# Gathers of a four-layer graph network: staged loops and a 12-batch ring against unrolled gathers, a 16-batch ring, and a ramp in PSUM

## What is computed

```
L0:  agg = segment_sum(relu(h[src]), dst); relu(relu((h+agg) @ W1 + b1) @ W2 + b2)
L1:  4 times: a = segment_sum((feat @ W[etype]^T + b[etype])[src], dst)
     feat = gru(a, feat)
L2:  twice: h = h @ W; out = segment_sum(h[src] * norm, dst) + b     (with self loops)
L3:  h = [x_i, x_j - x_i] @ W^T + b for each edge (i = dst, j = src)
     batch norm over all edges, leaky relu, mean over the edges of each dst
```

## Time and profile before

| | |
|---|---|
| median of three runs | 18,841.41 us (18,836.34 to 18,843.33) |
| profiled execution: its span, first to last instruction | 21,319.6 us |
| the profiled execution's own time outside the span | not given; its time is at least the span |
| POOL busy | 13,832.9 us, 65% |
| TensorE matmul / weight load busy | 10,388.0 us / 8,431.9 us |
| VectorE / ScalarE busy | 4,301.6 us / 813.3 us |
| DMA engines' mean busy share, moved | 0.09 + 0.04, 656 MB |

### The profile page before, as it was taken

How to read it: one execution, slowest core, us unless ns; L and a number is a source line. 1 busy time by engine, 2 the same in 40 slices (tenths; PEclk the granted TensorE clock), 3 DMA queues, 4 the chain that set the end, 5 groups by cost and what they waited for, 6 DMA issues and landing times.

```text
span 21319.6 us, 182142 instructions
## 1 busy us (share of the span) xinstructions
PE 10388.0 (49%) x40885; PEld 8431.9 (40%) x40886; DVE 4301.6 (20%) x4825; ACT 813.3 (4%) x2691; POOL 13832.9 (65%) x13640
## 2 busy tenths in 40 slices
PE   3333544445444463444634445443544445666689
PEld 2333333334333343333433333333433334656678
DVE  2111121112111121111211113111211112111168
ACT  0000000001000010000100001000000000000000
POOL 6766557774677746777377764676567764666677
PEclk5555555555555555555555555555555555555555
DMA  1111011110111111111111100111011111222222
GB/s 40 22 22 22 17 40 22 23 22 28 29 23 23 23 35 22 22 23 23 35 22 23 23 21 18 22 23 23 21 23 23 23 22 35 66 66 66 66 63 64
DMA packets 739325, 656.19 MB, mean 31 GB/s; under 512 B 457733, under 2 KB 467541, under 8 KB 738918
## 3 DMA queue, kind: packets, MB, share of 16 engines
q0 software_dynamic: 407168, 419.46, 9.4%
q1 hardware_dynamic: 332134, 236.47, 3.9%
HBM read 532.79 MB, written 122.26 MB: 31 GB/s over the span
## 4 chain that ended last, share of the span: by engine, by line
POOL 36%; another core or an unknown queue 25%; issue 19%; PE 15%; DVE 3%; DMA 1%; DVEq 1%; ACT 1%; POOLq 0%; ACTq 0%; SPq 0%
POOL HG L479 30%; PE ps L722 7%; POOL HG L461 5%; PE ps L875 2%; PE ps L803 2%; PE ps L719 1%; DVE OH L1012 1%; PE ps L766 1%; DMA HG<-tab_edge,STG 1%; PE ps L866 1%; DVEq L1005 1%; PE ps L835 0%; ACT RZ L643 0%; DMA HG<-tab_gin,STG 0%
## 5 line engine op out<-in xcount | busy, mean ns | idle before, releaser
L722 PE MATMUL ps<-HG,OH 128*128 (+2 forms) x26560 | 6212.0, 421 | 5999.6 <-issue 2938.7
L722 PEld LDWEIGHTS ps<-HG,OH 128*128 128x128 f32 x26560 | 5859.6, 329 | 6909.3 <-issue 6907.0
L479 POOL DMA_INDIRECT HG<-tab_gated,STG x6252 | 6424.0, 1028 | 2729.0 <-issue 2037.4
L479 POOL DMA_INDIRECT HG<-tab_gcn,STG x3126 | 3192.7, 1021 | 1386.1 <-issue 942.1
L1008 DVE TENSOR_TENSOR A<-A,ps 128x640 f32 (+1 forms) x1328 | 1091.9, 822 | 14010.3 <-issue 13934.3
L719 PE MATMUL ps<-ZERO 1*128 1x512 bf16 (+1 forms) x3819 | 1543.4, 535 | 3677.8 <-issue 2629.8
L461 POOL DMA_INDIRECT HG<-tab_gin,STG x1660 | 1712.9, 1032 | 750.3 <-issue 514.8
L461 POOL DMA_INDIRECT HG<-tab_edge,STG x1660 | 1587.9, 957 | 879.0 <-issue 490.4
L719 PEld LDWEIGHTS ps<-ZERO 1*128 1x128 bf16 x3819 | 338.8, 114 | 4260.3 <-issue 4199.7
L1012 DVE TENSOR_TENSOR OH<-IOTAR,DLOC 128x1280 f32<-128x1280 f32 x1328 | 2002.5, 1508 | 0.3 <-DVE A L1130 0.2
L875 PE MATMUL ps<-A,HG 128*128 (+1 forms) x3320 | 733.8, 353 | 601.6 <-issue 493.8
(11 more groups left out here) (157 smaller groups left out, 3002.8 us busy)
## 6 DMA issues: line engine op xcount, KB each, us to landing
HG<-tab_gated,STG POOLq DMA_INDIRECT x6252
A<-dloc_dram SPq DMA_DIRECT2D x166, 320.0 KB
kept<-HG SPq DMA_DIRECT2D x166, 320.0 KB
HG<-kept SPq DMA_DIRECT2D x166, 320.0 KB, 2.9
tab_gated<-TW SPq DMA_DIRECT2D x196, 256.0 KB, 2.0
HG<-tab_gcn,STG POOLq DMA_INDIRECT x3126
HG<-tab_gin,STG POOLq DMA_INDIRECT x1660
HG<-tab_edge,STG POOLq DMA_INDIRECT x1660
```

Source lines behind the costliest of these rows:

```text
L479: nc.gpsimd.indirect_dma_start(out=RINGF[:, at:at + D], out_offset=None, in_=table, in_offset=bass.IndirectOffsetOnAxis(ap=STG[:, h, u:u + ...
L722: return nc.tensor.matmul(ps[:, base:][:, bass.ds(place, width)], onehots_, rows_, start=False, stop=False, skip_group_check=True)
```

## The change

- The ramp for the one-hots is copied once into the last bank of PSUM (`ps_ramp`), and both comparisons read it, or a lane number (`ps_lane`), from there. `turned_onehots` is a tensor-tensor comparison now.
- The host lays out the index tables by row (`src_cols`, `type_cols`), so IDX and IDX4 are filled by two plain loads and some arithmetic; the indirect DMAs take their indices straight from them. STG, the staging copies and two of the three transposed tables are gone; the 13 fetches of the prologue bring only `dst`.
- All eight passes use one `gather` over 1,563 rows, unrolled (no hardware loop), into a ring of 16 batches. Before batch b it waits for the landing of batch b-2 and, from batch 16 on, for group b-5 (REACH is 11; `product`, or `e_joined` in the edge pass).
- In the first pass the ring's pitch is 65, with a column of ones for the counts, and the sums start from the normalised x. In the edge pass the join is ten additions, each from its ring slot (registers), into OH.
- The prologue normalises x and writes the first table before the edge rows are dealt with. Chunk buffers share one tensor (TEMP), lists lie in one tensor at four partitions.

```diff
-RING = 12
+RING = 16
+REACH = (GRP - 1 + NB - 1) // GRP + 1
...
+        ps_ramp = ps[:, 4096 - P:4096]
+        ps_lane = ps[:, 4095 - P:4096 - P]
...
+            def gather(n, table, index, pitch, rows, ring, freed, freed_before):
+                for b in range(BATCHES):
+                    h = b % 2
+                    if b >= 2:
+                        pool.wait_ge(rows[h], rows_before(ring, h) + (b // 2) * (16 * GRP))
+                        pool.sem_inc(pool_go, 1)
+                    if b >= RING:
+                        pool.wait_ge(freed, freed_before + min(b - RING + REACH, 2 * TRIPS))
+                        pool.sem_inc(pool_go, 1)
+                    for k in range(b * GRP, min((b + 1) * GRP, ROWS)):
+                        at = (k % RING_ROWS) * pitch
                         nc.gpsimd.indirect_dma_start(
                             out=RINGF[:, at:at + D], out_offset=None, in_=table,
-                            in_offset=bass.IndirectOffsetOnAxis(ap=STG[:, h, u:u + 1], axis=0)
+                            in_offset=bass.IndirectOffsetOnAxis(ap=index[:, k:k + 1], axis=0)
                         ).then_inc(rows[h], 16)
-                with pool.Fori(0, LAPS) as lap:
-                    for j in range(RING):
-                        batch(lap, j, GRP)
-                batch(LAPS, 0, ROWS - LAPS * RING_ROWS)
...
-            gather(0, tab_gin, rows_other, False)
+            gather_sums(0, tab_gin, IDX, D + 1, rows_other, 0)
...
-                gather_ring(step + 1, step, tab_gated, rows_gated)
+                gather_sums(step + 1, tab_gated, IDX4, D, rows_gated, step)
...
-                gather_ring(STEPS + 1 + k, STEPS + k, tab_gcn[k], rows_other)
+                gather_sums(STEPS + 1 + k, tab_gcn[k], IDX, D, rows_other, k + 1)
...
-            gather(LAST_PASS, tab_edge, rows_other, True)
+            gather(LAST_PASS, tab_edge, IDX, D, rows_other, 3, e_joined, 0)
...
-                def stage(i, h):
-                    nc.scalar.copy(STG[:, h, :], group_cols(IDX4, i, h)).then_inc(staged[h], 1)
...
             def onehots(cols, h):
-                return V.tensor_tensor(OH[:, h, :, :], IOTAR[:, :].unsqueeze(1).broadcast_to([P, GRP, P]),
+                return V.tensor_tensor(OH[:, h, :, :], ps_ramp.unsqueeze(1).broadcast_to([P, GRP, P]),
                                        cols.unsqueeze(2).broadcast_to([P, GRP, P]), ALU.is_equal)
...
-                V.tensor_scalar(OTS[:, h, :, :], DROW[:, h, :, :], VIS[:, 0:1], None, ALU.is_equal
-                                ).then_inc(e_turned, 1)
+                V.tensor_tensor(OTS[:, h, :, :], DROW[:, h, :, :], ps_lane.unsqueeze(1).broadcast_to([P, GRP, P]),
+                                ALU.is_equal).then_inc(e_turned, 1)
...
             def join(g, h, i):
+                rows = load_rows(g)
+                needed = dve.value_load(LOC[0:1, bass.ds(g * LPG + GRP, 1)], min_val=1, max_val=BATCHES)
                 dve.wait_ge(e_picked, g + 1)
...
-                dve.wait_ge(rows_other[h], rows_before(2, h, 1) + (i + 1) * (16 * GRP))
-                V.tensor_tensor(G[:, h, :, 0:D], G[:, h, :, 0:D], ps_u[:, h, 0:GRP, :], ALU.add).then_inc(e_joined, 1)
+                dve.wait_ge(batch_in, LAST_PASS * BATCHES + needed)
+                for u in range(GRP):
+                    ins = V.tensor_tensor(JOINED[:, h, u, 0:D], RINGF[:, bass.ds(rows[u], D)], ps_u[:, h, u, :],
+                                          ALU.add)
+                ins.then_inc(e_joined, 1)
...
             dve.wait_ge(typ_in, 32)
...
+            V.scalar_tensor_tensor(IDX4[:, :], IDX[:, :], float(TYPES), IDX4[:, :], ALU.mult, ALU.add
+                                   ).then_inc(idx_set, 1)
+            rescale(0, FEAT, SUMS)
 
             dve.wait_ge(rows_in, 16 * VT)
```

More of the change, by code:

```diff
@@ L24 @@
+import math
 from contextlib import ExitStack
@@ L204, in gnn_kernel @@
+        TOTAL = TEMP[:, 3 * GRP * P:3 * GRP * P + P]
+        JOINED = OH
+        LOADED, SCALED, ACTED = (cut(RINGF, k * 2 * GRP * D, [2, GRP, D]) for k in range(3))
         ps_g = ps[:, 0:3072].rearrange("p (h u f) -> p h u f", h=2, f=P)
@@ L239, in gnn_kernel @@
         typ_in = sem("typ_in")
-        staged = [sem(f"staged{h}") for h in range(2)]
         pool_go = sem("pool_go")
@@ L248, in gnn_kernel @@
         onehot = [sem(f"onehot{h}") for h in range(2)]
-        product = [sem(f"product{h}") for h in range(2)]
+        product = sem("product")
         group_added = sem("group_added")
@@ L412, in load_and_keep @@
                 keep(g - 2, h, i)
-            sp.wait_ge(mask_set, 1)
+            for s in range(2):
+                sp.wait_ge(edg_out[s], SLOT_DMAS[s])
             for h in range(2):
@@ L447, in _ @@
                 nc.gpsimd.indirect_dma_start(
-                    out=EB[:, g, :, :].rearrange("p k e -> p (k e)"), out_offset=None, in_=edges,
+                    out=EB[:, g, :], out_offset=None, in_=dst_rows,
                     in_offset=bass.IndirectOffsetOnAxis(ap=TJ[:, g:g + 1], axis=0)).then_inc(rows_in, 16)
-            def gather(n, table, rows, kept_):
-                def body(i, h, first):
-                    pool.wait_ge(staged[h], staged_before(0 if n == 0 else RINGS, h, min(n, 1)) + i + 1)
-                    pool.sem_inc(pool_go, 1)
-                    if kept_ and not first:
-                        pool.wait_ge(kept_out[h], i * 16)
-                        pool.sem_inc(pool_go, 1)
-                    for u in range(GRP):
-                        nc.gpsimd.indirect_dma_start(
-                            out=G[:, h, u, 0:D], out_offset=None, in_=table,
-                            in_offset=bass.IndirectOffsetOnAxis(ap=STG[:, h, u:u + 1], axis=0)
-                        ).then_inc(rows[h], 16)
-                groups(pool, body)
@@ L500, in pick, with gather_sums @@
                 chunks(pool, body)
-            pool.wait_ge(tabled, 4)
-            nc.gpsimd.iota(VNUM, [[GRP, 2 * TRIPS], [1, GRP]], base=0, channel_multiplier=0).then_inc(vnum_set, 1)
+            def gather_sums(n, table, index, pitch, rows, ring):
+                gather(n, table, index, pitch, rows, ring, product, n * 2 * TRIPS)
+            pool.wait_ge(idx_set, 1)
             pool.wait_ge(table_out, 16)
-            gather(0, tab_gin, rows_other, False)
+            gather_sums(0, tab_gin, IDX, D + 1, rows_other, 0)
             pool.wait_ge(mlp_in, 1)
-            pick(RUN_MLP, H, D, plus=SUMS)
-            with pool.Fori(0, STEPS) as step:
+            pick(RUN_MLP, SUMS, D)
+            for step in range(STEPS):
                 pool.wait_ge(group_added, (step + 1) * GK + 1)
@@ L564, in norm, with landed, come @@
                 root(n)
+            norm(0)
             act.wait_ge(cols_done, 1)
[L568 to L609 removed]
+            nc.scalar.copy(DL16, DVIS).then_inc(dloc_cast, 1)
+            act.wait_ge(turned, 1)
+            nc.scalar.copy(DLOC[:, :], ps[:, 0:VT * P]).then_inc(tabled, 1)
+            act.wait_ge(turned, 2)
+            nc.scalar.copy(BT[:, :], ps[0:VT, 2048:2048 + P]).then_inc(tabled, 1)
+            def landed(rows, ring):
+                def come(h, count):
+                    act.wait_ge(rows[h], rows_before(ring, h) + count * 16)
+                    act.sem_inc(batch_in, 1)
+                with act.Fori(0, BATCHES // 2) as i:
+                    for h in range(2):
+                        come(h, i * GRP + GRP)
                 come(0, IN_ROWS[0])
+            landed(rows_other, 0)
             def copied(run, dst, rows):
@@ L1208, in _ @@
             clear(SUMS)
+            for h in range(2):
+                dve.wait_ge(kept_out[h], TRIPS * 16)
+                dve.sem_inc(dve_go, 1)
             def edge_onehots(g, h):
```

355 lines of the change are left out of this document (148 added, 207 removed).

## The result

The changed kernel takes 18,141.06 us (median of four runs, 18,139.14 to 18,142.46), the kernel before 18,842.37 us (four runs, 18,836.34 to 18,844.52). The ratio is 0.9628 [0.9614, 0.9642]: 701 us saved, where 1,123 were forecast, and 41 us outside the range. (A ratio is that of the medians, with its 95% interval in brackets.) One thing must be said or the numbers don't fit together: executions of these kernels come in two kinds, a short one of about 18.8 ms for the kernel before and a long one of 21.3 to 21.7 ms, and the trace that stands ahead of the prediction (21,319.6 us) is of the long kind, while the runs timed above, and the trace of the changed kernel, are of the short one.

What follows compares the result with a forecast made beforehand. The kernel was taken as a chain of gathers on POOL, 12,698 at 1.25 us. Savings of 243 + 846 + 12 + 22 = 1,123 us from 18,841 gave 17,718, said as 17,700; range 16,600 to 18,100.

Steps and rivals of the forecast that it cites:

- 194 gathers fewer: First and last pass: 1,563 columns fetched in place of 1,660, at 1.25 us a gather, saving 243 us.
- clash of lines 1012 / 915: One-hot comparisons with both inputs in SBUF stretch gathers, 0.73 us each; ramp in PSUM saves all 846 us.
- clash of the edge pass's one-hot: Edge pass, line 1167: its one-hot gets the PSUM form too, saving 12 us.
- last stage: Stage without gathers: TensorE sets 5.15 us a group, so zero counted, at most 33 us.
- prologue: Before the first gather: first table no longer waits for edge rows or their transposes, saving 22 us.
- waits, staging, straight line: Batch starts and unrolled gathers: removed staging, shorter waits and straight-line code counted as zero in the runs.
- Hidden, by 2 us: Edge pass: VectorE needs at most 9.7 us a group, TensorE 9.8, POOL 11.8, so the new join costs nothing.
- TensorE's lateness belongs to the recording: POOL's 1,909 us of waits and 288 us of tails in the profile were taken as absent from ordinary runs.
- rival 1: Waits at batch starts are real in runs too: 15,521 us if all go, 16,620 if half are real; chance 0.22.
- the 282 us: Profiled span less waits and tails gives 19,123 us, still 282 over the runs' median; used against real waits.
- Rivals 2 and 3: 2: PSUM ramp changes nothing, 18,576 us, 0.13 with rival 4. 3: straight-line gathers are slower, 19,594 at 0.15 us each, 0.04.
- rival 4: Smaller straight-line loss, or only part of the clash removed: 18,000 to 18,500 us; chance 0.13 together with rival 2.

Runs made afterwards that it cites:

- l_before: Kernel before with TensorE made light: fixed block places, nine of ten ring products read a fixed tile, sums not computed; 18,845.72 us.
- l_after: Changed kernel with TensorE made light in the seven ring passes: fixed block places, nine of ten products read a fixed tile; 18,137.38 us.
- l_before_ramp: Kernel before with TensorE made light and the ramp of the one-hots read from PSUM; 18,368.03 us.
- the edit on GpSimd: Changed kernel with the edge pass's landed batches counted on GpSimd, ScalarE left with the squares; 18,064.63 us, 0.9587 of the kernel before.
- f1_after: Changed kernel run again unchanged, in long executions; 21,496.05 and 21,499.10 us, 1.0102 of the kernel before beside it.
- the light kernels: Four kernels, before or changed, ramp in SBUF or PSUM, with few TensorE register steps and sums not computed; 18,137.38 to 18,845.72 us.

## Why the prediction was wrong, by its own steps

The sum of the changes, from the spans of `l_before` (18,837.2) and `l_after` (18,135.3), 701.9 us apart, in us (0.9436 is a gather of the edge pass in `l_after`, 1,474.9 / 1,563):

```
term                               forecast   measured   from
194 gathers fewer                    243        242      194 x (0.944 + 0.305)
clash of lines 1012 / 915            846        459      busy times of l_before less l_before_ramp
clash of the edge pass's one-hot      12         38      1604.4 - 1660 x 0.9436
gathers of the first pass              0         13      (1585.6 - 1660 x 0.944) - (1481.2 - 1563 x 0.944)
last stage                             0         13      906.4 - 893.7
prologue                              22         22      84.1 - 61.7
waits, staging, straight line          0          4      the stretches between passes, 1480.9 - 1477.1
behind the edge pass                   0        -90      893.7 - 983.2
sum                                1,123        701
```

**The step that failed is the size of the clash**: "(1.028 - 0.95) x 6,252 = 488 us, (1.021 - 0.95) x 3,126 = 222, (1.032 - 0.95) x 1,660 = 136: 846 us", "the other 1,162 cost 0.73 us each". The mechanism was right: the changed ramp takes all of it away. The Trainium skill (SBUF — State Buffer, Who interferes with whom) infers that a comparison like this one doesn't stop descriptor generation; by that inference the edit would have been worth nothing, and the 519.2 and 477.7 us contradict it. Its rule that two inputs in SBUF contend with GpSimd's reads is not contradicted, since a gather reads its indices from SBUF: that descriptors can't be written meanwhile, as the prediction has it, was argued and not shown. But the price was read off an execution in which TensorE was late, while the same text argued that this lateness is not in the timed runs, and then "carried over to the median one for one". Both can't stand. If the waits are not there, VectorE's work starts elsewhere in POOL's cycle, and a price that hangs on that place is another one. The earlier trace rows had it all: the comparison began at 3,006.19, 0.78 us behind a gather's start, because POOL and VectorE both resumed on a late TensorE. An undisturbed group shows the place: TensorE starts 1.65 us behind the end of a batch's last gather, as the text itself counted, its twenty products take 4.53 us, the add follows 1.28 us later and the comparison 0.74 us behind that. This makes 8.20 us, and the seventh gather of the next batch starts at 0.305 + 6 x 1.249 = 7.80, so the comparison begins 0.40 us into a gather, not 0.78. (The 1.28 us is from the trace after; the trace before had only late groups there.) This term is 387 of the 422 us that are missing.

**The second failed step is the edge pass**, "Hidden, by 2 us". It compared busy times of engines per group, and these were right. It did not follow the order of the waits on one engine: ScalarE now takes a landing, a square, a landing, a square, so the square of a group stands behind a batch that lands later, though its own data is there. There are 157 batches but 166 groups; 154 squares are paired with landings, and twelve, with their sums at 8.53 us each, are left when the gathers end. The stretch behind them is 90 us longer, of which the edit on GpSimd gets 76 back.

**Smaller misses.** Line 1167 was priced at 12 us from a mean that had been rounded against 0.95; it is 38. The last stage was counted at zero because TensorE sets it, with a bound of 33; the comparison leaving the queue of the two vector engines gives 13. The first pass's gathers take 0.955 us in the kernel before, 0.011 more in each than elsewhere; why isn't known.

**"TensorE's lateness belongs to the recording"** was half right. It is not in the timed runs of this comparison, so rival 1 (15,521, or 16,620 for half of it) was rightly left aside, and the 282 us by which its account did not close pointed at the very term that was too large (846 less 459 is 387). And the gathers' busy time is indeed 419 us less in `l_before` than in the long trace (12,498.8 and 12,917.5). But the lateness isn't made by recording: the recorded executions of the short kind have none of it, and in the long kind a recorded execution is as long as the others of its kernel (21,496.05 and 21,499.10 us for `f1_after`).

**Rivals 2 and 3 did not happen.** The ramp is worth 478 to 519 us, not nothing. Straight-line code costs nothing: gaps of 0.305 us over 12,504 gathers, the fetch queue moved 126 packets where the kernel before had 13, and no gather waits for one. The rule of the Trainium skill on fetching ahead (Runtime: NRT & Kernel Launch, Instruction fetch mechanics), that crossing a block is mostly hidden, agrees with this; the prediction's own upper estimate of 240 us is not there. The time fell where rival 4 had it (18,000 to 18,500, given 0.13 together with rival 2), by another way than that rival named: no part of the clash was left, the clash was smaller. So that rival's place was hit by luck, and the forecast's own interval (17,500 to 17,900) was missed by 241 us.

What stays open is what makes an execution a long one. The register steps of 0.7 us and the stretches that end when POOL stops are seen in the traces, their cause is not; the light kernels never met that kind.

## What to carry over

The price of two engines meeting hangs on where in the cycle they meet. Before a mean from a trace is carried over to runs of another length, ask what the difference in length does to the starting places: work out one undisturbed group from landing to comparison, and take the price there. And where one in-order engine serves two streams, follow the order of its waits at the end of the stage; busy times don't show a tail.

## What was not expected of the hardware

- A gather that begins inside a comparison with both inputs in SBUF ends 0.81 to 0.83 us after the comparison, wherever it began, unless it began within the first 0.04 us; then it takes 0.94 to 0.96 us and the next one is held. With one input moved to PSUM the gather takes 0.944 us, at the same 1,280 values written (comparison 1.48 us).
- In some executions many of TensorE's register steps take about 0.70 us each while gathers run on GpSimd (6,869 against none for the same kernel), and the normal pace comes back about 5 us after POOL stops. The kernel before is then 2.4 to 2.9 ms longer; both kinds have been seen on one chip within three runs.
- Some 15,000 instructions in straight line on GpSimd cost nothing that a trace of 18 ms shows.
